# Perceiver block: the heads' tile steps written out, side work moved into other steps, z loads ahead of code loads, own-key scores per sequence

## The reference, cut to what matters

```python
# cross attention, two sequences' own rows put together per 128 rows
scores = einsum('bqd,bkd->bqk', q, concat([k_cache, k_new])) * scale
out    = einsum('bqk,bkd->bqd', softmax(scores), concat([v_cache, v_new]))
# heads
Q, K = rope(x @ W_Q + b_Q), rope(x @ W_K + b_K);  V = x @ W_V + b_V
z    = softmax(causal(Q @ K.T / sqrt(128))) @ V
out  = einsum('bqnd,ndm->bqm', z, W_O) + b_O
# feed-forward: silu(x @ gate) * (x @ up) @ down, weights = LUT[nibble] * scale
```

## Time and profile before

| | us |
|---|---|
| median of 3 runs (1452.6 to 1454.66) | 1453.63 |
| the profiled execution | 1456.01 |
| its span | 1454.2 |
| PE busy in the span | 1374.0 |
| DVE busy in the span | 982.8 |

### The profile page before, as it was taken

One profiled execution on the slowest core, in us unless ns is written; L12 is line 12 of the kernel. 1 busy time (PEld: TensorE's weight loads), 2 busy tenths in 40 slices (PEclk: granted clock), 3 DMA queues, 4 the chain that ended last, 5 costly groups with the idle time before them and its releaser, 6 DMA issues. The chain is left out here.

```text
span 1454.2 us, 25225 instructions
## 1 busy us (share of the span) xinstructions
PE 1374.0 (94%) x8788; PEld 803.0 (55%) x8788; DVE 982.8 (68%) x2187; ACT 512.3 (35%) x1221; POOL 445.6 (31%) x306
## 2 busy tenths in 40 slices
PE   8999999958899989999899999999989999999997
PEld 6666666425466646666566666664434434343433
DVE  6344344447777777777777767765869796969693
ACT  3222222322333333333333343330001483838281
POOL 0000000003333333333333333331402292929292
PEclk9999999988999999999899999999999999999999
DMA  8555555321100110001100020027852000000000
GB/s 327 212 206 200 207 192 190 140 105 58 59 29 29 34 68 29 29 29 43 58 29 29 14 88 29 29 94 194 237 158 92 1 2 29 0 29 0 29 1 30
DMA packets 59552, 122.01 MB, mean 84 GB/s; under 512 B 4328, under 2 KB 37864, under 8 KB 52840
## 3 DMA queue, kind: packets, MB, share of 16 engines
q1 hardware_dynamic: 59496, 121.27, 24.6%
HBM read 96.09 MB, written 25.17 MB: 83 GB/s over the span
## 5 line engine op out<-in xcount | busy, mean ns | idle before, releaser
L923 POOL TENSOR_TENSOR hd_rotated<-hd_products 64x512 f32<-64x512 f32 x64 | 112.8, 1763 | 718.6 <-DVE hd_products L1124 718.6
L183 PE MATMUL psum<-hd_xt_hi,hqk_hi 128*128 128x512 f16 x512 | 198.5, 388 | 4.9 <-DVE hd_xt_lo L1094 4.9
L184 PE MATMUL psum<-hd_xt_lo,hqk_hi 128*128 128x512 f16 x512 | 197.8, 386 | 0.0
L185 PE MATMUL psum<-hd_xt_hi,hqk_lo 128*128 128x512 f16 x512 | 197.3, 385 | 0.0
L1438 POOL TENSOR_TENSOR ff_part<-ff_part 128x512 f32<-128x512 f32 x88 | 127.5, 1464 | 99.7 <-DVE ff_part L1565 99.3
L183 PE MATMUL psum<-hd_wv_hi,hd_xt_hi 128*128 (+1 forms) x512 | 140.3, 274 | 5.0 <-DVE hd_wv_lo L1099 5.0
L1467 PE MATMUL psum<-ff_xt_hi,gu 128*128 128x512 f16 x352 | 133.9, 380 | 9.2 <-DVE ff_part L1565 3.3
L184 PE MATMUL psum<-hd_wv_lo,hd_xt_hi 128*128 (+1 forms) x512 | 140.3, 274 | 0.0
L185 PE MATMUL psum<-hd_wv_hi,hd_xt_lo 128*128 (+1 forms) x512 | 140.2, 274 | 0.0
L1468 PE MATMUL psum<-ff_xt_lo,gu 128*128 128x512 f16 x352 | 133.4, 379 | 0.0
L1565 DVE SCALAR_TENSOR_TENSOR ff_part<-psum,gu_scale,ff_part 128x512 f32<-128x512 f32 x176 | 119.8, 738 | 6.5 <-ACT ff_part L1515 3.6
(11 more groups left out here) (168 smaller groups left out, 2815.9 us busy)
## 6 DMA issues: line engine op xcount, KB each, us to landing
xa_kv_t<-in_ctx_t_dram SPq DMA_DIRECT2D x16, 1024.0 KB, 4.9
xa_kv<-in_ctx_dram SPq DMA_DIRECT2D x16, 1024.0 KB, 4.8
w_rows<-in_head_weights_dram SPq DMA_DIRECT2D x12, 1024.0 KB, 6.9
z_scratch<-hd_z_hi SPq DMA_DIRECT2D x32, 256.0 KB, 2.2
z_scratch<-hd_z_lo SPq DMA_DIRECT2D x32, 256.0 KB, 2.3
w_rows<-z_scratch SPq DMA_DIRECT2D x8, 1024.0 KB, 8.0
hqk_lo<-z_scratch SPq DMA_DIRECT2D x8, 1024.0 KB, 8.0
xn<-in_x_dram SPq DMA_DIRECT2D x8, 512.0 KB, 3.7
```

Source lines behind the costliest of these rows:

```text
L183: pe.matmul(out, lh, rh, start=(first and i == 0), stop=False)
L184: pe.matmul(out, lh, rl, start=False, stop=False)
L185: last = pe.matmul(out, ll, rh, start=False, stop=(final and i == k - 1))
L923: pool.tensor_tensor(rotated[0:HALF, w, 0, :], products[0:HALF, w, 0, :], products[0:HALF, w, 2, :], ALU.subtract)
```

## The change

Heads: the inner loop is gone. `for_each_step` now writes out the eight steps of a tile, so that columns of a pair are fixed numbers and not taken from a register; the outer loop over tiles 0 to 2 stays. The side work moves: the three parts of the next tile's normalization (statistics; inverse root; the four normalized blocks) stand on DVE in the steps of pairs 1, 2 and 3, between the maximum of the scores and the wait for the exponentials. `wo_hi` is one ACT operation at the end of the step of pair 3, `wo_lo` moves from POOL to DVE, into the same place of the step of pair 4, and SP's load of the next quarter (in the last tile that of the first z) stands behind the step of pair 4. POOL keeps its half of the rotary sums and nothing else. Where a tile's rows are turned, PE waits for them one by one between the passes of q0 and not for all four ahead of it. Merge: in each round SP issues z of half 0, then the codes, then z of half 1. Cross attention: new-key scores are computed per sequence (64 by 64, eight matmuls for four of 128 by 128), the mask and its load are gone, DVE takes only the maximum, ACT reads the scores from PSUM, and the new-key part of the probabilities is turned by two 64 by 64 matmuls and moved by two more ACT operations.

```diff
+    now = {k: v[:, 0:blocks] for k, v in stat.items() if k not in ("six", "meanvar")}
+    y = now["y"]
+    if 2 in parts:
+        n[0] = 2 * blocks
+        done(dve.tensor_scalar(now["var"], stat["meanvar"][:, 0:blocks, 1], LN_EPS, None, ALU.add))
+        inverse_root(dve, now, done)
+        done(dve.tensor_scalar(y, y, XS, None, ALU.mult))
+        assert n[0] == steps
+    if 3 not in parts:
         return
-    n[0] = 2 * blocks
...
@@ -394,8 +393,10 @@
                 banks.wait_room(pe, j, unit)
                 q, k_new, b = q_t[:, j % 2, :, :], k_t[:, j % 2, :, :], banks.bank(j, unit)
                 for k in range(KD):
-                    pe.matmul(psum[:, b, KV:KV + P], q[:, k, block_of(p)], k_new[:, k, block_of(p)],
-                              start=(k == 0), stop=(k == KD - 1), skip_group_check=True)
+                    for s in range(2):
+                        own = slice(p * P + s * S, p * P + (s + 1) * S)
+                        pe.matmul(psum[s * S:(s + 1) * S, b, KV:KV + S], q[:, k, own], k_new[:, k, own],
+                                  start=(k == 0), stop=(k == KD - 1), skip_group_check=True)
...
             def turn_probs(j, p):
                 unit = ("probs", p)
-                pe.wait_ge(exp_done, 2 * j + p + 1)
+                banks.wait_moved(pe, j, ("scores", p))
                 banks.wait_room(pe, j, unit)
-                for i in range(3):
-                    last = pe.transpose(psum[:, banks.bank(j, unit), block_of(i)], probs[:, p, block_of(i)], ident[:, :])
+                for i in range(2):
+                    pe.transpose(psum[:, banks.bank(j, unit), block_of(i)], probs[:, p, block_of(i)], ident[:, :])
+                for s in range(2):
+                    own = slice(s * S, (s + 1) * S)
+                    last = pe.matmul(psum[own, banks.bank(j, unit), KV + s * S:KV + (s + 1) * S], probs[own, p, KV:KV + S], ident[own, own],
+                                     start=True, stop=True, skip_group_check=True)
                 banks.fills(last, j, unit)
...
-                    act.activation(probs[:, p, :], probs[:, p, :], ACT.Exp, bias=low_top[:, p:p + 1], scale=XATTN_SCALE,
-                                   accum_out=total[:, p:p + 1]).then_inc(exp_done, 1)
+                    banks.moves(act.activation(probs[:, p, :], psum_of(j, ("scores", p), KV + S), ACT.Exp, bias=low_top[:, p:p + 1],
+                                   scale=XATTN_SCALE, accum_out=total[:, p:p + 1]), j, ("scores", p))
...
-                    banks.moves(act.activation(probs_t[:, p, :, :].rearrange("p a b -> p (a b)"), psum_of(j, unit, 3 * P), ACT.Copy), j, unit)
+                    act.activation(probs_t[:, p, 0:2, :].rearrange("p a b -> p (a b)"), psum_of(j, unit, KV), ACT.Copy)
+                    for s in range(2):
+                        own = slice(s * S, (s + 1) * S)
+                        last = act.activation(probs_t[own, p, 2, own], psum[own, banks.bank(j, unit), KV + s * S:KV + (s + 1) * S], ACT.Copy)
+                    banks.moves(last, j, unit)
...
-                    banks.moves(dve.tensor_tensor_reduce(probs[:, p, :], psum_of(j, unit, KV + P), mask[:, :], 1.0, LOWEST,
-                                                         ALU.add, ALU.max, top[:, p:p + 1]), j, unit)
-                    banks.wait_moved(dve, j, unit)
+                    dve.tensor_reduce(top[:, p:p + 1], psum_of(j, unit, KV + S), mybir.AxisListType.X, ALU.max).then_inc(top_found, 1)
+                    dve.wait_ge(top_found, 2 * j + p + 1)
                     dve.tensor_scalar(low_top[:, p:p + 1], top[:, p:p + 1], -XATTN_SCALE, None, ALU.mult).then_inc(low_top_ready, 1)
                 for p in range(2):
-                    dve.wait_ge(exp_done, 2 * j + p + 1)
+                    banks.wait_moved(dve, j, ("scores", p))
                     dve.reciprocal(inv_total[:, p:p + 1], total[:, p:p + 1]).then_inc(inv_ready, 1)
...
-                    step(Step(t * PAIRS + (PAIRS - 1), t + 1, PAIRS - 1, 0, turn_next=True))
+                for pair in range(PAIRS):
+                    ends = pair == PAIRS - 1
+                    step(Step(t, pair, turn_next=ends and not last_tile, proj=not (ends and last_tile), last_tile=last_tile))
             with eng.Fori(0, NT - 1) as t:
                 tile(t, False)
             tile(NT - 1, True)
-            step(Step(NT * PAIRS - 1, NT, PAIRS - 1, None, proj=False))
 
...
-            for_each_step(nc.sync, on_the_side, step)
+                if s.pair == WO_STEP:
+                    if s.last_tile:
+                        load_first_z()
+                    else:
+                        load_wo(s.t + 1)
+
+            for_each_step(nc.sync, step)
 
...
-                                       ALU.add).then_inc(added_pool, 1)
-
-            def on_the_side(t, last_tile):
-
-
-                pool.wait_ge(added_pool, t * (2 * PAIRS) + 4)
-                pool.wait_ge(wo_hi_done, t + 1)
-                pool.nop(nofuse=True)
-                pool.tensor_tensor(wo_lo[:, bass.ds(t * 4, 4), :].rearrange("p n m -> p (n m)"), w_rows[:, 0, :],
-                                   wo_hi[:, bass.ds(t * 4, 4), :].rearrange("p n m -> p (n m)"), ALU.subtract).then_inc(w_lo_done, 1)
-                pool.wait_ge(w_lo_done, t + (KD + 1))
-                pool.nop(nofuse=True)
-
-            for_each_step(nc.gpsimd, on_the_side, step)
+                                       ALU.add).then_inc(pool_rotated, 1)
...
             xt = [(xt_hi[:, k, :], xt_lo[:, k, :]) for k in range(KD)]
 
-            def project(s, w, half):
+            def project(s, w, half, turned=False):
                 unit = ("qk"[w], half)
                 banks.wait_room(pe, s.runs_proj, unit)
                 pair = s.next_pair
-                cols = bass.ds(pair * DH + half * (WIDE // 2), DH)
+                cols = slice(pair * DH + half * (WIDE // 2), pair * DH + half * (WIDE // 2) + DH)
                 left = [(hqk_hi[:, w * KD + k, cols], hqk_lo[:, w * KD + k, cols]) for k in range(KD)]
-                banks.fills(three_passes(pe, psum_of(unit), left, xt), unit)
+                for k in range(KD):
+                    if turned:
+                        banks.wait_moved(pe, s.runs_turn, ("x", k))
+                    last = three_passes(pe, psum_of(unit), left[k:k + 1], xt[k:k + 1], first=(k == 0), final=(k == KD - 1))
+                banks.fills(last, unit)
 
...
                                              rotated[:, 1, h, cols], start=True, stop=True, skip_group_check=True)
                     banks.fills(last, s.scores)
-                if s.turn_next:
-                    for k in range(KD):
-                        banks.wait_moved(pe, s.runs_turn, ("x", k))
                 if s.proj:
-                    project(s, 0, 0)
...
+                if s.pair == WO_STEP - 1:
+                    act.wait_ge(loaded[0], s.t * 16 + 32)
+                    act.activation(wo_hi[:, bass.ds(s.t * 4, 4), :].rearrange("p n m -> p (n m)"), w_rows[:, 0, :], ACT.Copy,
+                                   scale=WS).then_inc(wo_hi_done, 1)
 
             act.wait_ge(bias_scaled, 2)
             act.wait_ge(zeros_set, 1)
 
-            def on_the_side(t, last_tile):
-                act.wait_ge(loaded[0], t * 16 + 32)
-                act.activation(w_rows[:, 0, :], w_rows[:, 0, :], ACT.Copy, scale=WS).then_inc(wo_scaled, 1)
-                act.wait_ge(wo_scaled, t + 1)
-                act.activation(wo_hi[:, bass.ds(t * 4, 4), :].rearrange("p n m -> p (n m)"), w_rows[:, 0, :],
-                               ACT.Copy).then_inc(wo_hi_done, 1)
-            for_each_step(nc.scalar, on_the_side, step)
+            for_each_step(nc.scalar, step)
...
+                if s.pair in (1, 2, 3) and not s.last_tile:
+                    if s.pair == 1:
+                        dve.wait_ge(x_loaded, s.t * 16 + 16)
+                    layernorm(dve, s.t, xn, xn, stat, ln_step, xn_ready, parts=(s.pair,))
+                if s.pair == WO_STEP:
+                    dve.wait_ge(wo_hi_done, s.t + 1)
+                    if not isinstance(s.t, int):
+                        dve.nop(nofuse=True)
+                    dve.scalar_tensor_tensor(wo_lo[:, bass.ds(s.t * 4, 4), :].rearrange("p n m -> p (n m)"), w_rows[:, 0, :], WS,
+                                             wo_hi[:, bass.ds(s.t * 4, 4), :].rearrange("p n m -> p (n m)"),
+                                             ALU.mult, ALU.subtract).then_inc(w_lo_done, 1)
 
             def step(s):
                 if s.turn_next:
...
                     dve.tensor_scalar(low_top[:, :], top[:, :], -HEAD_SCALE, None, ALU.mult).then_inc(low_top_ready, 1)
+                    while_exponentials_run(s)
                     dve.wait_ge(exp_done, s.a + 1)
                     dve.reciprocal(inv_total[:, :], total[:, :]).then_inc(inv_done, 1)
                     dve.wait_ge(inv_done, s.a + 1)
```

(9 more changed lines are left out.)

109 lines of the change are left out of this document (46 added, 63 removed).

## The result

| | before | after |
|---|---|---|
| median, us | 1453.51 (1452.13 to 1454.66) | 1445.90 (1445.04 to 1448.01) |
| the profiled execution | 1456.01 | 1445.04 |
| its span | 1454.2 | 1443.2 |

Each median is over five runs. After over before is 0.9948, 95% interval 0.9935 to 0.9961: faster by half a per cent, where 1.4% was forecast, and 0.9 us outside the range.

The account below looks back on a forecast made before the run. PE's order was taken as the path. On the profiled 1456.01 us: heads -35, jumps +2, cross attention -7.5, merge +17.5, cold start +2, sum -21.0, 1435.0; median 2.4 lower, so 1432.6 us; own range 1424 to 1442, 8 in 10 1417 to 1445.

Parts of the forecast that it names:

- The jumps back: Heads, outer tile loop: each of two jumps back costs PE 0 to 5.7 us, 1 taken each, +2.
- this sign: Heads: the prediction called itself wrong if PE idles where a tile's loop jumps back.
- the cold start: Start of the feed-forward phase: low clock behind PE's idle time in the merge, +2 us, bounds 0 and +4.
- The bound of 5.7: Heads: upper bound in us per jump back, from PE's 5.69 us wait near the phase's start.
- The third rival: Heads: PE is held by fetching its code at each step, slower than before, 1480 us at 1.5 us a step; 4%.
- Heads without the jumps: Heads: PE's waits and slow clock go, -35 us, bounds -25 and -37.
- the second rival: Heads: only half is given back, as moved parts delay POOL's sums or low clock stays; about 1447 us; 14%.
- Cross attention: Cross attention: smaller new-key scores save 8.0 us, turning costs 0.5; -7.5 taken, bounds -8.5 and +8.
- the turning: Cross attention: one transpose of each pair becomes two small matmuls, 0.5 us in all, between 0 and 2.2.
- The bound of +8: Cross attention: upper bound in us if the small matmuls did not overlap in pairs, 0.25 us each.
- Merge: Merge: codes 3 behind z(3,0) delay DVE's chain 20.0 us; phase ends +17.5 us later, bounds +7.5 and +21.5.
- the first rival: Merge: the codes are no bound, the merge gives its 7 us and the cold start falls away; 1406 us; 11%.

Follow-up runs that it names:

- e3: The changed kernel with the outer loop over tiles written out too, so all four tiles are written out and no jump goes back; 1431.93 us, ratio 0.9863.
- e15: The changed kernel with pairs 2 to 6 as one step in an inner loop, all normalization in pair 1's wait for exponentials; 1449.18 us in one run.
- e8: e3, but PE waits for all four turned rows ahead of q0, as before the change; 1436.26 us in one run.
- e9: e3, with `wo_lo` a POOL subtraction again in pair 3's step and ACT scaling in place first; 1439.26 us in one run.
- e10: e3 with e2's order of loads: z(2,0), codes 2, codes 3; 1408.59 us, ratio 0.9690 to the kernel before.
- e11: e10 with the context transposes of both pairs ahead of the small matmuls that turn their own-key part; 1404.73 us, ratio 0.9671.
- e1: The changed kernel, but in the merge SP issues codes 2 and 3 ahead of the z pairs again; 1425.67 us, ratio 0.9816.
- e2: The changed kernel with z(2,0) first, then codes 2, codes 3 and the other z loads in the merge; 1421.36 us, ratio 0.9792.
- e4: The changed kernel with the cross attention of the kernel before; 1443.35 us, ratio 0.9936.
- e14: The changed kernel with pairs 4 to 6 in an inner loop (six steps written) and 96 more PE instructions ahead of it; 1451.54 us, ratio 0.9985.

## Why the prediction was right and wrong

**The jumps back: the step that failed.** The prediction put "0 to 5.7 for each of two jumps; I take 1 each, near the lower row, +2". They cost 6.5 each, above even the upper bound, 13.0 in sum; e3, which takes them away, has 13.0 us of these back in the same steps. The prediction had named this sign itself: "if it idles where a tile's loop jumps back". These 11.0 us more are the whole miss of 10.0 on the profiled executions; the other errors cancel but for 1.0, which is luck: 1.4 too much hoped from what lies ahead of the heads, 1.9 too much feared from the cold start, and half a microsecond in the heads and the merge. The low value rested on the old jumps, which showed no wait. That was a row of another case: before, the tile loop was 989 instructions and stayed held, and its 34 fetches on the page for a program of 8,866 instructions (34.6 pieces) say that nothing was fetched twice. The bound of 5.7 was an unrelated wait. Neither row spoke of a jump to code that is gone, and I should have let the range carry that. The Trainium skill, "Runtime: NRT & Kernel Launch", section "Instruction fetch mechanics", was right where I gave it only a microsecond: a taken branch whose target is not held stalls. It speaks of a target outside a window of two pages, though, and this case doesn't agree with that for PE: the loops of before, in 5 blocks, and of e15, in 6, jumped back without a fetch. The runs agree with its blocks of 256 instructions. Its 2048 instructions (eight blocks) are not what a loop may have: 1589 in 7 blocks were fetched again, 1288 in 6 were not. That the sequencer fetches the next page while it executes the current one, as the page says, might account for the missing blocks, but no run separates it.

The third rival, that each step is held by fetching, was wrong: straight code costs PE nothing (e3, 16,928 instructions on PE, every plain step 19.01).

**Heads without the jumps: right.** -35.2 came, -35 was said. The single prices fit too: statistics 2.47 (2.46), `xn` without POOL 1.91 (1.9), `wo_lo` on DVE 2.29 (2.3), turned rows 1.12 a turning (1.1, e8). e9 shows that moving `wo_lo` off POOL was needed, e15 that the parts had to be spread. That the second rival's time, about 1447, is close to what was measured is no support for it: the waits for probabilities and sums did go, as it said they would not.

**Cross attention: right in sign, a term mis-sized.** -7.5 was said, the phase ended 5.8 us earlier. A half tile went from 34.84 to 34.20. The scores saved more than forecast, 1.19 us a half tile where 1.0 was said; the turning cost 0.55 more, 4.4 in all, where 0.5 in all was said and 2.2 was the bound. The term had priced two small matmuls by the row of the heads' scores, where they stand among their like. The rows of e10 show four groups in 1.2 us where before one of six transposes took 0.66 to the next matmul. e11, with two groups, has 0.29 of it back, so about half of the price lies in going to and fro between the 128 by 128 transposes and the 64 by 64 matmuls; what makes the rest no run shows. The bound of +8 was also summed wrongly: eight small matmuls at 0.25 us are 2.0 a pair where the old ones took 1.04, +15 in all; nothing hangs on it here.

**Merge: right.** +17.5 was said, +17.2 came, by the chain that was given: codes 3 behind z(3,0), issued 20.1 us later in the phase than before (20.0 was said), DVE waiting (26.56 us), PE idle (24.20). e1 and e2 confirm it from both sides. e2's merge, 6.9 us shorter than before, gives the 7 us that the first rival hoped for, by an order of loads that the change did not have; in the change itself the codes were the bound.

**Cold start: too dear by a little.** +2 was said for the low clock at the start of the feed-forward phase. Its first tile is 1.25 us longer than before, and in e1 and e2, whose merge ends without the idle PE, the phase is 1.2 us shorter (303.2 against 304.4). That it is only 0.1 longer than before as a whole (304.3) comes of its last tile, which is 1.1 us shorter in every changed kernel of these; no run shows why.

## What to carry to other kernels

Writing a loop body out pays in instructions that can be placed, and nothing is lost as long as no jump leads back over it: either keep the loop small enough for its code to stay held (in these kernels 989 and 1288 instructions on PE were, 1589 and more were not), or write it out to the end. When a load is moved ahead in a queue to end one wait, look at what now stands behind the wait that this load itself has: the codes were needed by the second busiest engine and stood behind a load that waits for the first. The next best version is often an order in which the load that needs no wait goes first.

## What the runs showed of the hardware

- The cost of a jump back on PE depends on how many instructions lie ahead of the loop, anywhere in the program: 96 more at its start took 9.4 us off two jumps (13.0 to 3.6), and the cross attention, made cheaper by 5.8 us, made them dearer by 7.6.
- `nop` instructions written in the kernel took no room in the compiled program of PE.
- PE's granted clock can fall to the lower level for 3.4 us behind gaps as short as 1.8 and 2.9 us with five matmuls between them, and in e4 it did so behind a single gap of 2.00 us. Behind one of 2.16 us (e14) it did not.
